# One exponential per score slot over two PSUM banks, in an attention and mixture-of-experts kernel

## The reference

```python
q = l2norm(q) * q_scale
k = l2norm(k) * k_scale
sim = jnp.einsum("bhid,bhjd->bhij", q, k) * SCALE
sim = jnp.where(full_mask, sim, max_neg)
attn = jax.nn.softmax(sim.astype(jnp.float32), axis=-1)
out = jnp.einsum("bhij,bhjd->bhid", attn, v)
```

## Time and profile before

| what | value |
|---|---|
| median of 3 runs | 813.23 us (812.81 to 813.81) |
| profiled execution, its own time | 817.73 us |
| its span, first to last instruction | 816.0 us |
| granted TensorE clock, mean | 0.995 |
| busy: PE, DVE, ACT, POOL | 796.0, 500.2, 343.7, 342.4 us |

### The profile page before, as it was taken

One profiled execution on the slowest core, in us unless ns is written; L12 is line 12 of the kernel. 1 busy time (PEld: TensorE's weight loads), 2 busy tenths in 40 slices (PEclk: granted clock), 3 DMA queues, 4 the chain that ended last, 5 costly groups with the idle time before them and its releaser, 6 DMA issues.

```text
span 816.0 us, 13063 instructions
## 1 busy us (share of the span) xinstructions
PE 796.0 (98%) x4368; PEld 486.3 (60%) x4369; DVE 500.2 (61%) x925; ACT 343.7 (42%) x647; POOL 342.4 (42%) x252
## 2 busy tenths in 40 slices
PE   8999999999999999999999989999999999999987
PEld 4444355554555555455544547756558999999544
DVE  4887867777786878687776845647113333333334
ACT  3555456655655666566555321121112333333110
POOL 2100045868695876858596133203560000000563
PEclk9999999999999999999999999999999999999998
DMA  3105700000101010000020102781522223232343
GB/s 117 40 26 186 234 1 1 2 27 1 29 1 27 1 27 1 8 21 1 27 65 27 27 27 77 227 268 67 181 96 64 92 90 91 90 95 71 94 132 98
DMA packets 52838, 56.27 MB, mean 69 GB/s; under 512 B 9258, under 2 KB 47796, under 8 KB 52788
## 3 DMA queue, kind: packets, MB, share of 16 engines
q1 hardware_dynamic: 49556, 47.10, 18.5%
q0 software_dynamic: 3072, 8.39, 3.1%
q10 hardware_dynamic: 160, 0.14, 0.1%
HBM read 36.86 MB, written 18.67 MB: 68 GB/s over the span
## 4 chain that ended last, share of the span: by engine, by line
PE 88%; issue 6%; DVE 2%; ACT 2%; POOL 1%; DMA 0%; POOLq 0%; ACTq 0%; DVEq 0%
PE bank L1150 13%; PE bank L965 12%; PE bank L990 11%; PE bank L836 11%; PE bank L1215 10%; PE bank L1165 7%; PE bank L924 6%; PE bank L1224 5%; PE bank L970 4%; PE bank L1058 2%; PE bank L908 2%; ACT prob L1331 1%; PE bank L1205 1%; PE bank L985 1%; PE bank L1001 1%
## 5 line engine op out<-in xcount | busy, mean ns | idle before, releaser
L1331 ACT ACTIVATE prob<-bank,zero 128x512 f32<-128x512 f32 x256 | 161.2, 685 | 77.1 <-PE bank L970 74.8
L1549 DVE TENSOR_REDUCE mx<-bank 128x1 f32<-128x512 f32 x256 | 164.3, 686 | 43.4 <-PE bank L924 42.1
L723 POOL TENSOR_TENSOR acc<-acc,prob 128x1024 f32<-128x1024 f32 (+1 forms) x67 | 166.8, 2490 | 9.6
L990 PE MATMUL bank<-prob,vn 128*64 128x512 f32 x512 | 121.1, 602 | 0.0
L1150 PE MATMUL bank<-xfT,w12s 128*128 128x512 f32 x256 | 116.0, 598 | 0.8 <-ACT xfT L1392 0.8
L798 POOL DMA_INDIRECT slot_result<-slot_results,posi x32 | 30.8, 962 | 165.2 <-DMA slot_results<-yo 148.1
L1215 PE MATMUL bank<-xsT,w_slot 128*128 128x128 f32 x752 | 91.9, 275 | 1.0 <-ACT xsT L1426 1.0
L1215 PEld LDWEIGHTS bank<-xsT,w_slot 128*128 128x128 f32 x752 | 89.2, 191 | 6.0 <-ACT xsT L1426 1.6
L715 POOL TENSOR_TENSOR acc<-prob 128x1024 f32<-128x1024 f32 x16 | 41.4, 2587 | 121.5 <-ACT prob L1331 102.4
L1150 PEld LDWEIGHTS bank<-xfT,w12s 128*128 128x128 f32 x256 | 49.1, 193 | 50.8 <-issue 49.2
L1416 ACT ACTIVATE hidden_units<-bank 128x512 f32<-128x512 f32 x32 | 19.0, 597 | 135.4 <-PE bank L1150 123.4
(11 more groups left out here) (177 smaller groups left out, 1117.9 us busy)
## 6 DMA issues: line engine op xcount, KB each, us to landing
w12r<-in_L_ffn_routed_w SPq DMA_DIRECT2D x32, 256.0 KB
slot_rows<-zrow SPq DMA_DIRECT2D x47, 128.0 KB, 1.9
xsl<-slot_rows SPq DMA_DIRECT2D x47, 128.0 KB, 2.0
slot_results<-yo SPq DMA_DIRECT2D x47, 128.0 KB, 1.7
w3r<-in_L_ffn_routed_w SPq DMA_DIRECT2D x16, 256.0 KB
rec<-row_sum_reciprocals SPq DMA_DIRECT2D x30, 128.0 KB, 2.9
xin<-in_x SPq DMA_DIRECT2D x16, 128.0 KB, 2.1
w12s<-in_L_ffn_shared_w SPq DMA_DIRECT2D x2, 1024.0 KB, 7.1
```

What stands on the lines that cost most here:

```text
L723: g.tensor_tensor(acc[rows, c, :, :], acc[rows, c, :, :], prob[rows, n % PROBS, :, :], ALU.add).then_inc(summed, 1)
L990: last = mm_(o_bank(i, c)[rows, :], vn[:, kt, b, (2 * j + h) * DH:(2 * j + h + 1) * DH], prob[:, n % PROBS, h, :], start=(s == 0), stop=(s ...
L1331: a(prob[rows, held % PROBS, h, :], bank[2 * (n % 2) + h][rows, :], ACT.Exp, bias=bias[rows, :])\
L1549: v.tensor_reduce(mx[:, h, t, c:c + 1], ring_bank(u)[:, :], AX.X, ALU.max).then_inc(ring_used, 1)
```

## The change

The first four banks are now declared as two tensors of two neighbouring banks each; `bank[0]` to `bank[3]` are views of them, at the same places as before. `exponentials` waits for both heads of a slot and runs one ACTIVATE over both banks, 1024 values per partition in place of twice 512, and adds two to `probs_ready` at once. All other instructions, their order and their waits are as before; every line below the declaration is numbered two higher, from the ACTIVATE (L1332) on one higher.

```diff
-    bank = [es.enter_context(nc.psum_tensor(f"bank{i}", [P, 512], F32)) for i in range(8)]
+    score_banks = [es.enter_context(nc.psum_tensor(f"score_banks{i}", [P, 2, QC], F32)) for i in range(2)]
+    bank = [score_banks[i // 2][:, i % 2, :] for i in range(4)]
+    bank += [es.enter_context(nc.psum_tensor(f"bank{i}", [P, QC], F32)) for i in range(4, 8)]
...
-            for h in range(2):
-                act.wait_ge(scores_made, 2 * n + h + 1)
-                a(prob[rows, held % PROBS, h, :], bank[2 * (n % 2) + h][rows, :], ACT.Exp, bias=bias[rows, :])\
-                    .then_inc(probs_ready, 1)
+            act.wait_ge(scores_made, 2 * n + 2)
+            a(prob[rows, held % PROBS, :, :], score_banks[n % 2][rows, :, :], ACT.Exp, bias=bias[rows, :])\
+                .then_inc(probs_ready, 2)
```

## The result

The changed kernel takes **826.6 us** (median of 5, 825.11 to 826.79) against 813.23 (5 runs, 812.81 to 814.2): 1.69% slower, ratio 1.0169 with a 95% interval of 1.0157 to 1.0182. I had forecast 812.4, with 811.0 to 824.5 as the range. The first rival, "the port goes to POOL first", is what happened, and it cost more than I had priced. "The port" is the access to SBUF from which DVE's divides and tail sums and POOL's sums shut each other out.

A forecast was written before the change was run, and what follows sets the result against it. It took PE and a DVE-POOL chain from phase 3 to the next slot 0 as the bound, not ACT. Slot 2's 0.65 plus the first pair's 0.15 gave 0.8 us off 813.23: 812.4, range 811.0 to 824.5.

The forecast's parts named there:

- The first rival: Phase 3: POOL's L715 is served before DVE's L1606, which then waits; 818.4 to 825.0 us in all, chance 0.38.
- The length of the merged exponential: On ACT, one ACTIVATE of 1024 values takes 1113 ns against 1.27 us for two of 512, 0.15 us less.
- Slot 2, 0.09 a pair: PE's wait for ACT before L965 at slot 2 shrinks by 0.09 us in seven pairs, 0.65 us in all.
- L715 at 268.09. My case: DVE keeps its access from L1585 to L1606.: Phase 3: POOL's sum is ready 0.2 us earlier but still waits behind L1606; L970 of slot 0 unmoved; chance 0.47.
- The price of that rival: Second to seventh pair: of 1.8 us lost, slot 0 takes back 0.8 or nothing; 1.0 to 2.1 us a pair.
- The upper end of the range: Whole kernel: 824.5 us, set to take in nearly all of the slower rival's 818.4 to 825.0.
- The first pair: No L1606 in phase 3 there, so POOL's run, L1578 and the second pair's slot 0 come about 0.15 us earlier.
- The sum by that rule: Phase 3: the first to issue has the port, so L715 goes ahead of L1606; 818 to 825 us in all.

The follow-up runs named there:

- experiments 1 and 3: POOL's second run of sums also waits for DVE's L1585 (L1586 when changed): 1 in the changed kernel, 812.18 us; 3 in the kernel before, 811.98; both against 815.07.
- experiment 8: The kernel before, unchanged, run once more to profile another execution: 817.63 us against 817.24, ratio 0.9995.
- experiment 6: The changed kernel with exponentials merged at all slots but 9 and 11: 819.09 us against 819.43 for the kernel before, ratio 0.9987.

## Why the prediction was wrong

By its own steps:

- **The length of the merged exponential**: 1113 ns forecast, 1116 measured. It starts a little later behind PE, though: L970 of slot 11 ended at 266.85 and the exponential began at 266.96, now at 269.77 and 269.92. So a slot ends 0.12 us earlier and not 0.15.
- **Slot 2, 0.09 a pair**: right. L967 starts 0.34 behind L926 in the fourth pair, and with the port order restored (experiments 1 and 3) a pair is 0.10 shorter.
- **"L715 at 268.09. My case: DVE keeps its access from L1585 to L1606."** This is the step that failed. The 0.2 us of lead was forecast rightly (0.25 measured), and so was what it would do if POOL were served: L715 ends 2.23 behind L1585, the divide 0.55 behind that (2.22 and 0.54 measured). Only the winner was wrong. I took divides that won with POOL's row at most 0.01 us ahead (all six of that trace are so) as evidence that DVE holds on. They showed only that so small a lead doesn't count. DVE gives the port up between two of its instructions: L717 waited while L1586 ran and was served before L1607.
- **The price of that rival**: 1.0 to 2.1 a pair forecast, 2.1 measured at full clock. The sum took the dear end because POOL was first again at L1579, as said above. One term of it was short: PE's round writes two banks, so L926 waits for both L1540 and not the first alone, and came 31.05 behind slot 0 where it had been 29.36, 1.7 late and not 1.5.
- **The upper end of the range** failed on a term I did not have: the lower clock after the new wait, 3.9 us (three pairs of 48.2 against 46.9). The rival's own sum, five pairs of 2.1 (one kept the port), less 0.5 for the pair that did and the first, is 10.0; with 3.9 for the clock it is 13.9, against 13.7 in the profiles and 13.4 in the medians.
- **The first pair**: 0.15 forecast, 0.3 measured (41.22 to 40.90). In the kernel before, slot 11's first exponential began 0.40 behind the end of L970 in this pair and 0.11 to 0.12 behind it in the others; I had not seen that in the earlier trace rows. The merged one began 0.15 behind it, and L717 ended 0.35 earlier in its pair.

The Trainium skill, SBUF — State Buffer, section "Who interferes with whom", gives the port to the one that issues first. The runs bear it out: in the ten traces where the divide follows L1585 directly, POOL had it every time with a lead of 21 ns or more in the recorded starts (21 to 24, 112 to 143, 230 to 260 ns), DVE with POOL 17 ns ahead or less, or behind. So by recorded starts POOL needs a lead of some 20 ns, which the rule does not say. The sum by that rule was the better one.

Not settled: in the third pair of the changed kernel the exponential of slot 11 began 0.42 us behind the end of L972 and not 0.14 to 0.15, and these 0.27 are more than POOL's whole lead, so that DVE was first. It is no chance of one execution: the traces of all five kernels with every slot merged have it in the third pair (0.42 to 0.43), and the six with two exponentials at slot 11 have a like delay in the first pair alone (0.40 and not 0.12). What holds ACT there the traces don't show; that the third pair kept the port, and five were lost and not six, was luck. Nor do the runs say why the clock fell after some of the waits of 1.82 us and not after others.

## What to carry to other kernels

When two engines exclude each other on something (here DVE and POOL with operands in SBUF), look at which asks first at each meeting, not at busy times: a faster instruction off the critical path can turn a won meeting into a lost one, and all that stands behind the loser on its engine pays. Where the trace shows two such starts within a few hundredths of a microsecond, the order is luck; a wait that pins it costs next to nothing, and here its runs were 0.4% faster and spread over 3.6 us and not 9.5. Before calling a change bad, pin the orders it upset: the same merged exponential is worth 0.10 us a pair gained, or 2.1 to 3.4 lost.

## What the runs showed that I had not expected

- The meeting is decided by about 20 ns: a lead of 17 ns lost and one of 21 won, in one execution (experiment 8); 16 lost and 24 won in another (experiment 6).
- TensorE, after 1.82 us of waiting, ran 3.4 us at 1.2 GHz in three of five such waits, which made a stall of 2.1 us one of 3.4.
- One ACTIVATE over two banks runs at the rate of one bank: (1116 - 685) / 512 = 0.84 ns a value.
